# Half-precision copy of the values moved from GpSimd to ScalarE, with all five engines' orders laid out anew

## The reference, cut to what matters

```python
qkv = einsum('btc,dc->btd', x, W_qkv); z = einsum('btc,dc->btd', x, W_z)
qkv_c = sum(pad(qkv)[:, j:j+T, :] * conv_w[:, j] for j in range(4))
q, k = _l2norm(q-part of qkv_c), _l2norm(k-part of qkv_c); v = v-part of qkv_c
def step(S, inp):                       # over the 256 tokens
    q_t, k_t, v_t, b_t, d_t = inp
    Sk = einsum('bhi,bhipj->bhpj', k_t, S)
    dv = b_t[..., None] * (v_t - Sk)
    S = S * d_t[:, :, None, :, None] + einsum('bhi,bhpj->bhipj', k_t, dv)
    return (S, einsum('bhi,bhipj->bhpj', q_t, S))
out = out * rsqrt(mean(out * out) + eps) * norm_w
y = einsum('btd,cd->btc', out.reshape(..) * silu(z), W_out)
...
x = x + ga * y;  h = _layernorm(x, axis=-1) * (1 + cb) + sb
x = x + gb * (sparsify_2to4(silu(h @ w_gate) * (h @ w_up)) @ w_down)
```

## Time and profile before

| | |
|---|---|
| median of three runs | 1903.93 us |
| the profiled execution | 1904.61 us |
| span of its trace | 1902.9 us |
| TensorE (PE) busy | 1819.9 us, 96% |
| VectorE (DVE) busy | 1760.3 us, 93% |
| ScalarE (ACT) busy | 1662.2 us, 87% |
| GpSimd (POOL) busy | 1579.1 us, 83% |
| last chain, by engine | POOL 54%, issue 19%, PE 15%, DVE 9%, ACT 2% |

### The profile page before, as it was taken

The page is one execution under the profiler, slowest core; times in us unless marked ns, Lnnn a source line. Parts: engine busy times, 40 slices in busy tenths (PEclk is TensorE's granted clock), DMA queues, the critical chain, the costliest instruction groups (busy, mean ns, idle before and its releaser), DMA issues.

```text
span 1902.9 us, 64596 instructions
## 1 busy us (share of the span) xinstructions
PE 1819.9 (96%) x24518; PEld 1499.0 (79%) x24518; DVE 1760.3 (93%) x2905; ACT 1662.2 (87%) x3207; POOL 1579.1 (83%) x1403
## 2 busy tenths in 40 slices
PE   7799999999999999999999999999999999987999
PEld 6577788887788887788887778888778888876888
DVE  7899999999999999999999999999999999986987
ACT  7599999999999999999999999999999999985332
POOL 5588899888989988889988889998989998883452
PEclk9899999999999999999999999999999999998999
DMA  3111010101010110111010101001010100022000
GB/s 124 36 31 41 25 48 25 42 25 45 21 47 25 29 38 24 42 25 47 25 42 25 41 25 47 25 22 45 25 42 25 47 25 20 25 85 78 21 15 23
DMA packets 36595, 69.89 MB, mean 37 GB/s; under 512 B 7868, under 2 KB 16572, under 8 KB 33988
## 3 DMA queue, kind: packets, MB, share of 16 engines
q1 hardware_dynamic: 36292, 65.77, 11.1%
HBM read 62.86 MB, written 2.90 MB: 35 GB/s over the span
## 4 chain that ended last, share of the span: by engine, by line
POOL 54%; issue 19%; PE 15%; DVE 9%; ACT 2%; POOLq 1%; DMA 0%; DVEq 0%; SPq 0%; ACTq 0%
PE bank L729 13%; POOL e_b L563 7%; POOL kq L516 6%; POOL a_lo L578 6%; POOL pt L523 6%; POOL b_le L553 6%; POOL osc L591 5%; POOL w L508 4%; DVE ae L1936 3%; POOL a L610 3%; POOL ri L530 3%; DVE yl L1966 2%; POOL solv L625 2%; POOL solv L632 2%; PE bank L732 1%
## 5 line engine op out<-in xcount | busy, mean ns | idle before, releaser
L1911 DVE SCALAR_TENSOR_TENSOR cc<-bank,wc,cc 128x510 f32<-128x510 f32 (+2 forms) x768 | 535.9, 741 | 2.6
L729 PE MATMUL bank<-h,w 128*128 128x512 f16 (+1 forms) x1920 | 424.2, 362 | 7.3 <-POOL w L508 5.7
L729 PEld LDWEIGHTS bank<-h,w 128*128 128x128 f16 x1920 | 178.0, 99 | 144.2 <-DVE zg L2014 8.7
L516 POOL TENSOR_TENSOR kq<-cc,kq 128x1024 f16<-128x1024 f32 x64 | 137.0, 2141 | 127.1 <-ACT kq L1467 127.1
L1518 ACT ACTIVATE invT<-bank 128x512 f16<-128x512 f32 x384 | 234.8, 611 | 4.9 <-PE bank L729 4.9
L1966 DVE TENSOR_TENSOR yl<-bank,mask 128x512 f16<-128x512 f32 x320 | 218.9, 684 | 3.9 <-PE bank L729 3.9
L1513 ACT ACTIVATE inv<-bank 128x512 f16<-128x512 f32 x320 | 195.2, 610 | 11.2 <-PE bank L729 10.9
L1433 ACT ACTIVATE cc<-bank,wc 128x512 f32<-128x512 f32 x256 | 175.1, 685 | 20.8 <-PE bank L729 17.8
L729 PE MATMUL bank<-w,h 128*128 128x256 f16 x1536 | 190.9, 275 | 0.0
L729 PE MATMUL bank<-w,goT 128*128 128x256 f16 x1536 | 188.6, 273 | 0.0
L732 PE MATMUL bank<-ident,cc 128*128 128x128 f32 x1024 | 159.0, 278 | 24.0 <-ACT v L1495 22.4
(11 more groups left out here) (234 smaller groups left out, 5499.1 us busy)
## 6 DMA issues: line engine op xcount, KB each, us to landing
inv<-ident_store SPq DMA_DIRECT2D x64, 256.0 KB, 2.6
invT<-ident_store SPq DMA_DIRECT2D x64, 256.0 KB, 2.6
w_raw<-in_wh SPq DMA_DIRECT2D x15, 1032.0 KB, 5.0
out<-sol SPq DMA_DIRECT2D x16, 128.0 KB, 1.7
v<-in_x SPq DMA_DIRECT2D x3, 512.0 KB, 3.8
moving<-rank_store SPq DMA_DIRECT2D x64, 8.0 KB
standing<-rank_store SPq DMA_DIRECT2D x64, 8.0 KB
w_raw<-in_wgate SPq DMA_DIRECT2D x1, 1024.0 KB, 5.0
```

Of the source, the lines that this page charges most:

```text
L516: gp.tensor_tensor(kq16[:, 1].rearrange("p i t s -> p i (t s)"), cc[:, 0:2], kq16[:, 0].rearrange("p i t s -> p i (t s)"), ALU.subtract).t ...
L729: return mm(o_, l_, r_, start=start, stop=stop, skip_group_check=True)
L1911: V.scalar_tensor_tensor(dst, src, wc[:, par(s), i, 3 - j:4 - j], dst, ALU.mult, ALU.add).then_inc(sig(f"conv{i}"), 1)
```

## The change

The function `values_half` goes from GpSimd's program to ScalarE's, where it is an activation `Copy` of the same 512 elements per partition, placed behind the level-3 copies. Besides, the order inside `body` is changed on GpSimd, TensorE, ScalarE and VectorE. On GpSimd and VectorE a part of this is only that the border between two bodies is drawn elsewhere (`gate_output`, `split_weights`, `z_gate`, `decayed_queries`, `first_inverse`). In the last bodies that moved border does alter the order. The diff:

```diff
--- before.py
+++ after.py
@@ -618,13 +618,6 @@
                                  .broadcast_to([P, U, HP]), odds(a1[:, ring(s)]), ALU.mult).then_inc(sig("it"), 1)
 
 
-            def values_half(s):
-                n = N(s)
-                need(pool, "vv", n * 2 + 2)
-                need(pool, "b_ps", n * 2 - 1)
-                gp.tensor_copy(v16.rearrange("p (g n) -> p g n", g=BG),
-                               v[:, ring(s)].rearrange("p (g c) v d -> p g c (v d)", c=CH)[:, :, 0, :]).then_inc(sig("v16"), 1)
-
             def rest_half(s):
                 n = N(s)
                 need(pool, "rr", n * 4 + 4)
@@ -659,28 +652,29 @@
                 key_columns(s0)
                 masked_beta(s0)
                 decay_beta(s0)
-                split_weights(s0)
 
             def body(s0, s1, s2, s3):
                 if s0 and N(s0) == 0:
                     return first_body(s0)
-                if s1:
+                if s3:
+                    gate_output(s3)
+                if s1:
+                    split_weights(s1)
                     unit_system(s1)
                     first_inverse(s1)
-                    low_half(s1)
                 if s3:
                     output_scale(s3)
+                if s1:
+                    queries_rest(s1)
+                if s3:
                     scaled_output(s3)
+                if s1:
+                    low_half(s1)
+                if s2:
+                    rest_half(s2)
                 if s0:
                     pairs_low(s0)
-                if s2:
-                    rest_half(s2)
-                if s0:
                     key_norm(s0)
-                if s1:
-                    queries_rest(s1)
-                    values_half(s1)
-                if s0:
                     key_columns(s0)
                     masked_beta(s0)
                     decay_beta(s0)
@@ -689,15 +683,12 @@
                         add_input(j)
                     for j in range(TL):
                         hidden_rstd(j)
-                if s2:
-                    gate_output(s2)
-                if s0:
-                    split_weights(s0)
-                if s1 and (not s0):
                     hidden_low(0)
                     hidden_low(1)
 
             def last_bodies(s0, s1, s2, s3):
+                if s2:
+                    gate_output(s3)
                 output_scale(s3)
                 scaled_output(s3)
                 if s2:
@@ -1128,12 +1119,13 @@
                 if s2:
                     base_values(0, s2)
                 if s1:
+                    key_cross(s1)
                     need(pe, 'iv', N(s1) + 1)
                     turn_values(0, s1)
-                    key_cross(s1)
+                if s2:
+                    base_residue(0, s2)
+                if s1:
                     level_left(0, s1)
-                if s2:
-                    base_residue(0, s2)
                 if s0:
                     bank_project(2, s0, s2)
                     project(2, s0)
@@ -1143,10 +1135,9 @@
                     need(pe, 'vv', N(s0) * 2 - 1)
                     turn_keys(s0)
                 if s1:
+                    level_right(0, s1)
                     level_rows(1, s1)
-                    level_right(0, s1)
-                if s2:
-                    first_output(s2)
+                if s2:
                     key_state(s2)
                 if s1:
                     need(pe, 'kx', N(s1) + 1)
@@ -1156,22 +1147,22 @@
                     bank_project(3, s0, s2)
                     project(3, s0)
                 if s2:
+                    first_output(s2)
+                    base_values(1, s2)
+                if s1:
+                    level_left(1, s1)
+                    level_right(1, s1)
+                if s2:
                     query_state(s2)
-                if s1:
-                    level_right(1, s1)
-                    level_left(1, s1)
                 if s0:
                     need(pe, 'vv', N(s0) * 2)
                     turn_queries(s0)
-                if s2:
-                    base_values(1, s2)
-                if s0:
                     key_key(s0)
-                if s2:
-                    base_residue(1, s2)
                 if s3:
                     bank_turn_output(0, s0, s3)
                     turn_output(0, s3)
+                if s2:
+                    base_residue(1, s2)
                 if s1:
                     level_rows(2, s1)
                 if s3:
@@ -1199,16 +1190,16 @@
                     project_output(0, s3)
                 if s1:
                     level_left(3, s1)
+                    level_right(3, s1)
                 if s3:
                     bank_output(1, s0)
                     project_output(1, s3)
                 if s1:
-                    level_right(3, s1)
                     level_rows(4, s1)
                     bank_z(0, s1)
                     z_rows(0, s1)
+                    level_left(4, s1)
                     level_right(4, s1)
-                    level_left(4, s1)
                     bank_z(1, s1)
                     z_rows(1, s1)
                     level_rows(5, s1)
@@ -1525,6 +1516,13 @@
                 A(yl[HP:P, YL, :, 0:HP], bL[0][HP:P, :].rearrange("p (u s) -> p u s", s=HP), ACT.Copy,
                   scale=-1.0).then_inc(sig("yt"), 1)
 
+            def values_half(s):
+                n = N(s)
+                need(act, "vv", n * 2 + 2)
+                need(act, "b_ps", n * 2 - 1)
+                A(v16.rearrange("p (g n) -> p g n", g=BG),
+                               v[:, ring(s)].rearrange("p (g c) v d -> p g c (v d)", c=CH)[:, :, 0, :], ACT.Copy).then_inc(sig("v16"), 1)
+
             def base_kept(c, s):
                 n = N(s)
                 need(act, "b_ps", n * 2 + c + 1)
@@ -1668,8 +1666,8 @@
                 if s2:
                     base_kept(0, s2)
                 if s1:
+                    cross_kept(s1)
                     values_turned(0, s1)
-                    cross_kept(s1)
                     inverse_left(0, s1)
                 if s2:
                     first_kept(s2)
@@ -1677,19 +1675,17 @@
                     squares(0, s0)
                 if s1:
                     inverse_right(0, s1)
+                if s0:
+                    last_tap(2, s0)
+                    pairs_high(s0)
+                    last_tap(3, s0)
                 if s2:
                     first_output(s2)
-                if s0:
-                    pairs_high(s0)
-                    last_tap(2, s0)
-                    last_tap(3, s0)
                 if s1:
                     values_turned(1, s1)
-                    if not s0:
-                        gate_weights_high()
-                if s2:
+                if s2:
+                    base_kept(1, s2)
                     query_part(s2)
-                    base_kept(1, s2)
                 if s1:
                     inverse_left(1, s1)
                     inverse_right(1, s1)
@@ -1711,16 +1707,19 @@
                     output_squares(s2)
                 if s1:
                     inverse_left(3, s1)
+                    inverse_right(3, s1)
+                    values_half(s1)
+                    if not s0:
+                        gate_weights_high()
                 if s0:
                     split_weights(s0)
                 if s1:
-                    inverse_right(3, s1)
                     z_tanh(0, s1)
                     inverse_left(4, s1)
+                if s0:
+                    high_half(s0)
+                if s1:
                     inverse_right(4, s1)
-                if s0:
-                    high_half(s0)
-                if s1:
                     z_tanh(1, s1)
                     level_rows_last(s1)
                     if not s0:
@@ -2153,21 +2152,15 @@
                 squared_norms(1, s0)
                 level_masks_diagonal()
                 dve.wait_ge(sig("mask_steps"), 5)
+                decayed_queries(s0)
                 decayed_keys(s0)
 
                 dve.wait_ge(sig("gate_dma"), 32)
+                first_inverse(s0)
 
             def body(s0, s1, s2, s3):
                 if s0 and N(s0) == 0:
                     return first_body(s0)
-                if s2:
-                    z_gate(0, s2)
-                if s1:
-                    decayed_queries(s1)
-                if s2:
-                    z_gate(1, s2)
-                if s1:
-                    first_inverse(s1)
                 if s0:
                     convolve(0, 1, s0)
                     convolve(0, 2, s0)
@@ -2191,9 +2184,6 @@
                     if not s0:
                         gated(0)
                         gated(1)
-                    level_rows(1, s1)
-                if s0:
-                    squared_norms(0, s0)
                 if s2:
                     second_rest(s2)
                     if not s0:
@@ -2201,10 +2191,14 @@
                         gated(3)
                 if s0:
```

(16 more changed lines are left out.)

6 lines of the change are left out of this document (3 added, 3 removed).

## The result

The changed kernel takes 1913.9 us (median of four runs, 1913.02 to 1917.38) against 1903.43 for the kernel before (four runs): ratio 1.0057, 95% interval 1.0039 to 1.0074. I had forecast 1900.2 and a range up to 1909.0. One execution of the kernel before, timed beside experiments a to d, took 2208.48 us at a granted clock of 0.78 and is left out everywhere. The profiled execution took 1913.05 us with a span of 1911.3, 8.4 us more than the span before.

The account below looks back on a forecast made before the run. The prediction took chain G through GpSimd to bound the steps, chain B 0.07 to 0.1 us shorter. Steady steps -5.0 us and end +1.3 gave -3.7, so 1900.9 profiled and 1900.2 us median; range 1895.5 to 1909.

Parts of the forecast that it names:

- single waits: Steady steps: `pairs_low` wait gone, norms wait new, `z_gate` wait of 0.36 us gone, idle before `z_tanh` 0.1 to 0.2.
- The price of the copy: ScalarE, ahead of `split_weights` and `z_tanh`: the added copy hides in idle time and costs nothing.
- its price without cover: ScalarE's copy, if TensorE's wait-free run to `z_rows` did not hide it: 0.6 us in each step.
- The rival that ScalarE becomes the bound: Steady steps: the added copy finds no idle time, 38 us more, 1942 us; chance 0.02.
- first step: the steady part: Steady steps: closing at 25.63 to 25.66 us, 25.9 at new heads, 0.08 less on average; -5.0 us over 62 steps.
- Slack 0.1 to 0.3 us: TensorE ahead of `second_values`: second `base_residue` ends about 988.4, before VectorE reaches `base_rest` at 988.78, so reordering costs nothing.
- chain G: Loop through GpSimd, `pairs_low` to `gate_output` to next `convolve`: sets the 25.70 us step shown; `gate_output` gains only 0.1 us.
- chain B: Loop without GpSimd: VectorE to second `base_rest`, TensorE to `z_tanh`, ScalarE to `last_tap`; could close at 25.63 us.
- second step: the start: Start of the kernel: moved by under 1 us either way.
- third step: the end: Last bodies: `z_gate` waits for `gate_output` behind `hidden_low`, delaying `base_rest(0)`; +1.3 us, bounds 0 to +4.3.
- Upstream 2.03 us and "about 0.9 more": End: VectorE regains 2.03 us on `hidden_normed`, about 0.9 from ScalarE's gate weight copies; `hidden_low` ends near 1727.7.
- the rival of ScalarE's dense run: Steady steps: late `second_kept` delays `second_output` and chain B; with 0.2 us a step, 1912.6 us; chance 0.20.

Follow-up runs that it names:

- a: Changed kernel with GpSimd's `low_half` behind `pairs_low` instead of ahead of `rest_half`, except in the last body; 1911.51 us, ratio 1.0036 to the kernel before.
- d: Changed kernel with the old order in its last body: `gate_output` ahead of `hidden_low`, `z_gate` behind the gate weights; 1914.34 us, ratio 1.0051 to the kernel before.
- b: Kernel before with `values_half` on ScalarE behind `inverse_right(3)`, which moves ahead of `split_weights`; 1940.19 us, ratio 1.0186.
- e: Kernel before with only `values_half` moved to ScalarE, between `inverse_left(3)` and `split_weights`; 1911.49 us, ratio 1.0036.
- i: Kernel before with `values_half` on ScalarE behind `inverse_right(3)`, both ahead of `split_weights`, and TensorE's `level_right(3)` ahead of `project_output(1)`; 1903.3 us, ratio 0.9995.
- f: Changed kernel with TensorE's `base_residue(1)` ahead of `turn_output(0)` again; 1911.54 us, ratio 1.0037 to the kernel before.
- g: Changed kernel with `low_half` late except in the second step, VectorE's old order partly restored in the first two bodies, and d's end; 1903.93 us, ratio 0.9992 to the kernel before.

## Why the prediction was wrong

*Right.* All that it said of single waits: GpSimd no longer waits for the high halves, the norms are waited for instead, `z_gate`'s wait shrinks, `first_output` on ScalarE does not hold up `second_output`, the idle time before `z_tanh` falls from 0.68 to 0.17 us, the two `hidden_normed` at the end fall from 2.76 to 0.72 us. The price of the copy was nothing, and its price without cover, 0.6 us a step, is near the 0.63 of b, where a part of it is the wait of 0.81 us for `level_right(3)`. The rival that ScalarE becomes the bound, which leaned on the Trainium skill (Perfetto Trace Analysis, Identifying the Most-Contended Engine), didn't come true. b and e, which move the copy and hardly anything else to the busier engine, are slower, as that page's rule would have it; but what they lose are waits for TensorE, and in i the same move costs nothing. And GpSimd, with the lowest busy share, was the one that could not take `low_half`, `queries_rest` and `rest_half` in front of `pairs_low`.

*Wrong, first step: the steady part.* The failed step is the sentence on TensorE, "`base_residue` ... ends at about 988.4. Slack 0.1 to 0.3 us". It took `pairs_low` to end near 986.8, 10.97 us into the step. In ordinary steps of after it ends at 11.21, and `base_residue` begins 12.46 us into the step, ending near 13.1 where 988.4 would be 12.6. The 10.97 had been found from the high halves alone; I had listed what leaves GpSimd's way from `pairs_low` to `gate_output` (3.4 us) and never added up the way from `gate_output` round to `pairs_low`, to which the same 2.7 us of `queries_rest` and `rest_half` had gone. A change that moves work on an engine from one half of a loop to the other must be summed over both halves. Also left out of the same sentence: `turn_output(0)`, moved between `key_key` and `base_residue(1)` (f: 0.11 us a step when it is put back), and `last_tap(2)`, which now waits for TensorE ahead of the high halves. Experiments a and f cut this chain from its two sides and give 0.17 and 0.11 us a step. The sum had -5.0 us for 62 steps; the 59 steps measured +3.29.

*Wrong in the reason, too.* Even where the chain is cut, relief of GpSimd is worth only 0.03 us a step, and nothing of it is seen in ordinary steps. The prediction had chain G alone holding the steps at 25.74, and chain B as next. i relieves chain G and keeps 25.73: a third chain, VectorE up to the second `base_rest`, then `second_output`, `output_sums`, `gate_output`, was as long but for these 0.03, and ScalarE's `cross_kept` holds it up at its start. I had its last link in hand (the sums end at 995.58, `gate_output` starts at 995.76) and took 0.08 us for the hand-over where i and g show 0.17, so that a gain of 0.1 seemed left; and I never asked what bounds the sums.

*Wrong, second step: the start.* "Under 1 us either way" was not worked out. It measured +3.30. In d, which leaves the start as after has it, it is +2.4; in g, with three pieces put back, +0.96. One piece is the swap of `decayed_queries` and `decayed_keys` in the first body: TensorE's wait for GpSimd's `unit_system` ends 14.06 us behind the first `pairs_low`, in before 12.90. The 0.9 us between after and d go with the clock (last section).

*Wrong, third step: the end.* Forecast +1.3 with bounds 0 to 4.3; the trace has +4.3. The step's own working holds: `z_gate` waits for `gate_output` behind `hidden_low`, and costs what it costs. Mis-sized were two terms. Upstream 2.03 us and "about 0.9 more" were to be gained, and 0.3 came. `hidden_low`'s pair, forecast to end near 1727.7 in the old frame, which is 1731.7 with the 3.96 us by which the changed kernel was late at its last `first_inverse`, ended at 1734.2. The 2.03 us of `hidden_normed` came back, but the first `base_rest(1)` of this body is 16.1 us behind that `first_inverse`, where it was 12.9 behind. Of these 3.3 us 1.0 are there at `rest_half`, at 1711.09 where it was at 1706.11: before it the first two `gated` of VectorE took 3.10 us beside GpSimd's `low_half`, which now stands there. Another 1.4, by which after is later than d, go with the clock; the rest I have not traced. The second term is the gate weights, taken at 2.48 us from the earlier trace rows: they took 4.19, beside `scaled_output`. With both, `base_rest(0)` is 5.4 us late where 1.3 were forecast, and 4.3 are left at the last `output_sums`. The prediction drew on the port rule of the Trainium skill (SBUF — State Buffer, Terms) to take a collision away at this place and did not ask where the moved GpSimd operations would make new ones. The rule holds in both: 2.31 us of `low_half` against 2.35 us more for `gated` (0.75 in before), 1.93 of `scaled_output` against 1.71 more for the weights.

*The rivals.* The time came out near that of the rival of ScalarE's dense run (1912.6), by none of its mechanism.

## What to carry to other kernels

When operations are moved round a loop, close every chain again, over the whole step and both sides of the place from which they were taken; waits that vanish say only that one link has gone. Count how many chains end within a tenth of a microsecond of the longest before you price the relief of one. A new order spread over engines is one edit: the swap on TensorE cost 0.63 us a step without its half on VectorE, ScalarE's copy 0.15 to 0.63 without TensorE's move. And the first and the last pass of a pipelined loop deserve their own sum, here 7.6 of the 10.9 us.
